# A fused cross-attention and mixture-of-experts layer: four engine programs written as one list each, in a new order

## What is computed

```python
x = x + xattn(layernorm(x), ctx, ctx, W_Q, W_K, W_V, W_O)   # 8 heads of 16
#   scores = q k^T / 4;  attn = softmax(scores, axis=1)       # over the HEADS
x = x + ffn(layernorm(x), Wr, br, W1, b1, W2, b2)
#   logits = x Wr + br; top 2 of 8; gates = softmax of the two
#   h = relu(x W1[e] + b1[e]);  y = sum_e gates[e] * (h W2[e] + b2[e])
```

## Time and profile before

| | before |
|---|---|
| median of 3 runs | 207.93 us (207.81 to 209.05) |
| profiled execution | 208.05 us |
| its span in the trace | 206.2 us |
| PE busy | 193.4 us (94%) |
| DVE busy | 171.9 us (83%) |
| ACT busy | 133.8 us (65%) |
| POOL busy | 120.1 us (58%) |
| granted TensorE clock | 90% or more of full in each of 40 slices |

### The profile page before, as it was taken

How to read it: one execution, slowest core, us unless ns; L and a number is a source line. 1 busy time by engine, 2 the same in 40 slices (tenths; PEclk the granted TensorE clock), 3 DMA queues, 4 the chain that set the end, 5 groups by cost and what they waited for, 6 DMA issues and landing times.

```text
span 206.2 us, 4730 instructions
## 1 busy us (share of the span) xinstructions
PE 193.4 (94%) x1600; PEld 170.7 (83%) x1600; DVE 171.9 (83%) x460; ACT 133.8 (65%) x318; POOL 120.1 (58%) x154
## 2 busy tenths in 40 slices
PE   6999997989998999999999999998999899979995
PEld 6449965976987799978899789978997799779994
DVE  5799986999999989998898989897999979356543
ACT  6257768957776568766777776776667665444541
POOL 6123959998699729376944967196729773220010
PEclk9999999999999999999999999999999999999999
DMA  6968789345024505041242324140000000000000
GB/s 167 275 214 208 174 268 259 106 135 153 5 102 127 156 26 174 10 150 33 102 102 78 103 103 105 60 119 3 0 24 4 2 0 14 15 3 0 27 2 29
DMA packets 20360, 18.74 MB, mean 91 GB/s; under 512 B 1776, under 2 KB 18800, under 8 KB 20336
## 3 DMA queue, kind: packets, MB, share of 16 engines
q1 hardware_dynamic: 19904, 18.04, 30.6%
q10 hardware_dynamic: 432, 0.39, 0.6%
HBM read 11.88 MB, written 6.55 MB: 89 GB/s over the span
## 4 chain that ended last, share of the span: by engine, by line
PE 66%; DVE 19%; issue 7%; POOL 6%; ACT 1%; DVEq 0%; POOLq 0%; ACTq 0%
PE y_ps L449 20%; PE h_ps L434 12%; PE misc_ps L390 6%; PE score_ps L371 6%; DVE acc L1026 4%; PE h_ps L379 4%; DVE attn L943 4%; PE score_ps L359 3%; PE score_ps L348 2%; DVE shift_m L935 2%; PE score_ps L292 2%; PE score_ps L434 2%; DVE ln_stats L895 1%; POOL gatesD L1244 1%; PE misc_ps L399 1%
## 5 line engine op out<-in xcount | busy, mean ns | idle before, releaser
L703 ACT ACTIVATE hT<-h_ps,b_sb 128x256 f32<-128x256 f32 x118 | 49.4, 470 | 31.1 <-PE h_ps L434 31.1
L449 PE MATMUL y_ps<-w_sb,hT 128*128 128x128 f32 x508 | 67.7, 276 | 0.0
L449 PEld LDWEIGHTS y_ps<-w_sb,hT 128*128 128x128 f32 x508 | 62.8, 192 | 1.8 <-issue 0.7
L1212 POOL TENSOR_TENSOR half_sum<-e_sb 128x512 f32<-128x512 f32 x28 | 37.6, 1344 | 21.0 <-ACT e_sb L675 21.0
L943 DVE TENSOR_TENSOR attn<-e_sb,e_rcp 128x1024 f32<-128x1024 f32 x32 | 48.2, 1511 | 0.6 <-ACT e_rcp L686 0.6
L935 DVE TENSOR_REDUCE shift_m<-score_ps 128x128 fp32r<-128x1024 f32 x32 | 38.5, 1211 | 0.3 <-PE score_ps L348 0.3
L675 ACT ACTIVATE e_sb<-score_ps 128x1024 f32<-128x1024 f32 x32 | 32.6, 1022 | 7.9 <-PE score_ps L371 5.9
L434 PE MATMUL h_ps<-x1T_hi,w_lo 128*128 128x256 f32 x118 | 37.4, 320 | 0.2
L1026 DVE SCALAR_TENSOR_TENSOR acc<-y_ps,gates,acc 128x128 f32<-128x128 f32 x96 | 28.9, 342 | 7.7 <-PE y_ps L449 6.1
L434 PE MATMUL h_ps<-x1T_hi,w_hi 128*128 128x256 f32 x118 | 32.9, 281 | 0.0
L434 PE MATMUL h_ps<-x1T_lo,w_hi 128*128 128x256 f32 x118 | 31.9, 281 | 0.0
(11 more groups left out here) (122 smaller groups left out, 276.9 us busy)
## 6 DMA issues: line engine op xcount, KB each, us to landing
k_scratch<-k_parts SPq DMA_DIRECT2D x14, 256.0 KB, 2.6
k_stack<-k_scratch SPq DMA_DIRECT2D x14, 256.0 KB, 4.0
q_stack<-q_scratch SPq DMA_DIRECT2D x28, 128.0 KB, 2.7
q_scratch<-q_parts SPq DMA_DIRECT2D x7, 256.0 KB, 2.1
w_sb<-in_w SPq DMA_DIRECT2D x1, 1024.0 KB, 6.3
out_y<-y_out SPq DMA_DIRECT2D x7, 128.0 KB, 1.8
x_all<-in_x SPq DMA_DIRECT2D x1, 768.0 KB, 6.4
ctxT<-in_ctx_t SPq DMA_DIRECT2D x1, 640.0 KB, 7.2
```

The source lines that it names most:

```text
L449: mm = nc.tensor.matmul(product(j, t), hT[:, j % 2, c, t * P:(t + 1) * P], w2_sb[:, e * HC + c, :], start=(c == 0), stop=(c == HC - 1))
L703: op = nc.scalar.activation(hT[:, j % 2, c, :], hidden(j)[:, c * S:(c + 1) * S], ACT.Relu, bias=b1_sb[:, e * HC + c:e * HC + c + 1])
L1212: nc.gpsimd.tensor_tensor(half_sum[:], e[:, 0:HQ // 2], e[:, HQ // 2:HQ], ALU.add).then_inc(sum_step, 1)
```

## The change

Every engine's `beginning()` and `period()` are replaced by one list, `program()`, over all eight batches, and the places of steps within the lists differ. No step is added or taken away, and no step's own instructions change, apart from the places of the b2 addition:

```diff
-    PERIODS = B + 5
-    B2_AFTER = 2
+    B2_AFTER = (2, 4, 3, 3, 3, 2, 0, 5)
...
-                if e == B2_AFTER + 1:
+                if e == B2_AFTER[b] + 1:
                     dve.wait_ge(b2_added, b + 1)
...
-                dve.wait_ge(gated, E * b + B2_AFTER + 1)
+                dve.wait_ge(gated, E * b + B2_AFTER[b] + 1)
```

SP's list: the load of `w1` goes behind the stack loads of batch 1, that of the later contexts behind those of batch 2:

```diff
             sp.dma_start(wr_sb[:], wr).then_inc(small_in, 16)
-            sp.dma_start(w1_sb[:], w1.rearrange("e d h -> d e h")).then_inc(w1_in, 16)
             spill_k(1)
             spill_q(1)
             load_k_stack(1)
             load_q_stack(1)
-            sp.dma_start(ctxT[:, 3:B, :], ctx_t[3:B].rearrange("b d s -> d b s")).then_inc(ctx_rest_in, 16)
+            sp.dma_start(w1_sb[:], w1.rearrange("e d h -> d e h")).then_inc(w1_in, 16)
```

On PE, the calls around the last `attend_values`. Before, the last two periods put it between `expert_up(6, 3)` and `expert_down(6, 2)`; now it stands between `expert_up(6, 1)` and `expert_up(6, 2)`:

```diff
+                expert_down(6, 0)
+                expert_up(6, 1)
+                attend_values(7, logits_made, 7)
+                expert_up(6, 2)
+                project_out(7, heads_taken, 8)
+                expert_down(6, 1)
```

More of the change, by code:

```diff
@@ L615, in _ @@
+                expert_up(7, 7)
+                gated_b2(7, logits_made, 8)
+                expert_down(7, 6)
+                expert_down(7, 7)
             pe.wait_ge(ident_made, 1)
@@ new lines, in program @@
+                add_residual(3)
+                ln2(3)
+                transpose_gates(2)
+                add_expert(2, 1)
+                k_lo(6)
+                add_expert(2, 2)
+                normalize(4, 0)
+                head_max(5, 0)
+                head_max(5, 1)
+                add_expert(2, 3)
+                add_b2(2)
+                add_expert(2, 4)
+                normalize(4, 1)
+                normalize(4, 2)
+                x1T_low(3)
+                add_expert(2, 5)
@@ new lines, in program @@
+                add_expert(2, 6)
+                take_logits(3)
+                normalize(4, 3)
+                q_lo(6)
+                head_max(5, 2)
+                choose_experts(3)
+                head_max(5, 3)
+                add_expert(2, 7)
+                normalize(5, 0)
+                make_gates(3)
+                add_expert(3, 0)
+                add_expert(3, 1)
+                transpose_gates(3)
+                add_residual(4)
+                ln2(4)
+                normalize(5, 1)
@@ new lines, in program @@
+                k_lo(7)
+                add_expert(3, 2)
+                add_expert(3, 3)
+                normalize(5, 2)
+                add_b2(3)
+                add_expert(3, 4)
+                x1T_low(4)
+                head_max(6, 0)
+                head_max(6, 1)
+                take_logits(4)
+                add_expert(3, 5)
+                add_expert(3, 6)
+                q_lo(7)
+                choose_experts(4)
+                normalize(5, 3)
+                normalize(6, 0)
@@ new lines, in program @@
+                add_expert(3, 7)
+                make_gates(4)
+                head_max(6, 2)
+                transpose_gates(4)
+                add_expert(4, 0)
+                head_max(6, 3)
+                add_expert(4, 1)
+                add_residual(5)
+                ln2(5)
+                add_expert(4, 2)
+                add_expert(4, 3)
+                add_b2(4)
+                normalize(6, 1)
+                head_max(7, 0)
+                head_max(7, 1)
+                x1T_low(5)
@@ new lines, in program @@
+                transpose_gates(6)
+                add_residual(7)
+                ln2(7)
+                add_b2(6)
+                add_expert(6, 1)
+                add_expert(6, 2)
+                x1T_low(7)
+                add_expert(6, 3)
+                add_expert(6, 4)
+                add_expert(6, 5)
+                add_expert(6, 6)
+                take_logits(7)
+                choose_experts(7)
+                add_expert(6, 7)
+                make_gates(7)
+                add_expert(7, 0)
@@ L1186, in _ @@
             ln1_end(0, 0)
[L1187 to L1189 removed]
+            program()
         @block.gpsimd
```

878 lines of the change are left out of this document (539 added, 339 removed).

## The result

The change made no gain. Over 20 executions each, the changed kernel takes 209.44 us (median; 208.36 to 211.29) and the kernel before 208.51: ratio 1.0053, 95% interval 1.0032 to 1.0074, so half a per cent slower. The profiled execution took 208.75 us, its span is 206.9 us, and 1.85 us lie outside the span as before. The forecast was 200.0 us.

The account below looks back on a forecast made before the run. VectorE and TensorE, both nearly full, bound the kernel until batch 7's last `normalize`, then TensorE alone. 43.7 + 120 + 3.9 = 167.6 us; the tail gives span 198.2, plus 1.85 outside: 200.0 us, range 195.0 to 206.0.

Parts of the forecast that it names:

- Step 1: VectorE from batch 0's last `normalize` to batch 1's: stretch falls from 22.8 to 15.1 us, starting at about 28.6 us.
- M1: End of batch 1's last `normalize`: 49.0 us before, forecast 43.7 us.
- Step 2: From batch 1's last `normalize` to batch 7's: 120 us of VectorE work plus 3.9 us of waits, ending at 167.6 us.
- M7: End of batch 7's last `normalize`: 176.1 us before, forecast 167.6 us.
- So the work stays at about 120 us: VectorE's work between the last `normalize` of batches 1 and 7: work put off returns, about 3.0 us goes out.
- the other 3.9 us of waits: VectorE's waits for expert products, `project_out` and `q` between batch 1's and 7's last `normalize`: all kept.
- The bias: `add_b2` waiting for the gated bias: 3.2 us of VectorE waits go, and 1.0 us of TensorE idle in the tail.
- the waits only move: Rival: two nearly full engines hand each other every delay, so removed waits return elsewhere; 205.6 us, chance 0.22.
- TensorE's count: TensorE's list from `attend_values(1)` to `attend_values(7)`: 119 us against 123.9 us available, so 5 us to spare.
- Step 3: Tail from the last `attend_values` to TensorE's end: 27.4 us where 26.1 passed before; TensorE ends at 195.2 us.
- Step 4: `w1` load lands after 6.3 us; ACT waits up to 0.8 us, costed at nothing because VectorE's other work covers it.
- The collisions: Rival: `normalize` meets GpSimd head sums more often, slower above mean 1.93 us, worst case 213.2 us; chance 0.08.

Follow-up runs that it names:

- a_bias_late: Changed kernel with the bias chain's place undone (transposes of batches 3 to 6 close ahead of `add_b2`, `ln2_end` ahead of `block_gates`): 215.87 us, ratio 1.0388.
- a_pe_cut: Changed kernel with 4.8 us less TensorE work: experts 1, 2, 4, 5 of batches 3 to 7 skip the low-half x1T pass: 207.59 us, ratio 0.9971.
- a_nr_both2: Changed kernel, GpSimd head sums replaced by non-reading memsets of 3.26 us, plus a 0.4 us VectorE memset ahead of each of 28 `normalize`: 204.84 us, ratio 0.9847.
- a_max4: Changed kernel with `head_max` reading four of the eight heads, 16.9 us less of it on VectorE: 207.30 us, ratio 0.9948.

## Why the prediction was wrong

**Step 1 (M1 at 43.7 us) was near.** The start of the stretch was right: the two `head_max` begin at 28.56 us, 28.6 was said. The stretch took 44.95 - 28.64 = 16.3 us in place of 15.1. Waits were not the cause: the two listed there are 0.75 and 0.15 us, near the 0.7 us said. `onehot` took 0.94 us where it takes 0.19 undisturbed, and two cheap instructions that split the router's weights, some 0.4 us, had not been counted.

**Step 2 (M7 at 167.6 us) failed,** by 8.9 us: 1.3 from M1, 3.85 in the sentence "So the work stays at about 120 us", and 3.8 in the sentence on the other 3.9 us of waits, "I keep them all".

- *The bias.* "The wait goes on VectorE, and on TensorE" is right. No row of `add_b2` is left above, and TensorE's waits for `gatesD` fell from 3.6 us (five times, whole run) to 0.3 us (once). Set at 3.2 + 1.0 us in the sum, it is worth 6.4 us in the new order by `a_bias_late`.
- *The work.* VectorE's work from M1 to M7 is 123.85 us, from 118.93 counted in the same way. Of these 4.9 us more, 3.4 are `make_gates`: its first and third instruction took 3.63 + 2.26 us over six batches, before 1.28 + 1.17. The step took off 0.9 us "if `make_gates` runs without POOL beside it", and it runs beside GpSimd's sums in four of these six batches. Another 2.6 us are `add_expert`, of which 14 calls are followed straight by the next one in place of 5, and neighbouring calls cost more (below). Some smaller steps took less.
- *The waits.* They sum to 7.7 us in place of 3.9. That is what the rival "the waits only move" said; its price of 205.6 us was too low, since it put back at most the waits that had been removed. Of its mechanism, two full engines that hand each other every delay, `a_pe_cut` shows one direction: TensorE's waits for VectorE grow as its own work shrinks.
- *TensorE's count.* "That is 119 us, against 123.9 us" was off. Without reads, and with 0.2 us of its waits listed, TensorE takes 168.22 - 43.97 = 124.25 us from `attend_values(1)` to `attend_values(7)`. Its expert steps take 76.8 us there from start to start, where 74.5 were counted, and `scores` and `subtract_max` 23.2 in place of 20.2; the other terms held. The 5 us to spare were not there, and the span of 198 us that the forecast asked for is the one that this list reached with no late result from batch 1 on. So the forecast asked that nothing be late on a list without slack.

**Step 3 (the tail) was near.** From the start of `attend_values(7)` to the end of the span it is 206.9 - 177.07 = 29.8 us in place of 27.4 + 3.0 = 30.4, and TensorE has no wait in it. The 27.4 us were added to 26.1 us that the chain gave, and in TensorE's timeline the same stretch of before is 26.6 us long. In the changed kernel the timeline gives 203.76 + 0.61 - 177.07 = 27.3 us, so the tail grew by 0.7 us and not by 1.3.

**Step 4 (`w1`) was right.** ACT waits 0.6 us for it, at most 0.8 was said, although landing took 7.8 us in place of 6.3. The cover held: between 20.1 and 28.6 us VectorE has no wait in its timeline, with `head_max` and `normalize` back to back.

**The collisions** were set at 0.08, with a worst case counted from a mean `normalize` of over 1.9 us. The mean rose only from 1511 to 1549 ns, so by that test the rival was refuted, and the test was too narrow. It looked at one instruction's mean, while the small ones of `make_gates` and GpSimd's own sums were hit too, and it asked only for the growth, while the collisions already in the kernel before cost 4.6 us there. What the new order changed is what the collisions cost: 9.0 us in it, 4.2 us in the old order with the bias early, although the reads lengthen VectorE's instructions alike. Without them the excess falls by 10.9 us in the new order (23.1 to 12.2) and by 11.3 us in the old one (19.3 to 8.0). In the old order TensorE waits for nothing from 92 to 177 us; in the new one delays of VectorE still reach it there.

Without the reads, the new order meets the forecast's marks: M1 lies at 43.58 us and M7 at 167.70. That is luck as far as the parts go. VectorE has 114.5 us of work and 9.6 us of waits between them, where 120 and 3.9 were said, and the length of the stretch is that of TensorE's list.

The Trainium skill, page "SBUF — State Buffer", section "SBUF: two separate sides", says that an instruction that loses the port pair blocks until the other's end. The rows at 45.20 and 46.34 agree within 0.02 us. The same section of the Trainium skill says that a VectorE instruction with two SBUF inputs is affected only by a GpSimd instruction that reads SBUF. The mean `normalize` of 1256 ns without reads of the head sums agrees, and so do the two of these 32 that still took 1.71 and 1.76 us: GpSimd's split of `w1`, which reads, was under way as they began.

What stays open: which delays, besides that of `make_gates`, make up the half of the 9.0 us that `a_nr_both2` does not give back, and which places of the new order, one by one, make it wait where the old one does not. Ahead of the tail, neither VectorE's nor TensorE's amount of work alone sets its pace, as `a_max4` and `a_pe_cut` show.

## What to carry to other kernels

Before a reordering is costed by waits removed, count the busiest engine's own list to the end: if its sum is the forecast, the forecast holds only if nothing is ever late. Try a single edit that takes an engine's wait off the path (here the bias's transposes some steps earlier) alone first: it gained 4.5 us in the old order, and inside a new order of everything its gain was lost again. And test which engine sets the pace by taking a few microseconds off each: the share that comes back (0.88 of TensorE's in one order, 0.39 in the other, 0.06 to 0.14 of VectorE's) says more than busy shares, which are nearly the same in the two orders (94 and 95%, 85 and 85%).

## What the runs showed of the hardware

- A short VectorE instruction can pay as much for a GpSimd instruction that reads as a long one: 0.90 us in place of 0.16 for 128x2 numbers. With GpSimd's memsets in place of the head sums' reads, 28 of the 32 `normalize` took 1.21 to 1.23 us, but that short one (a tensor with a constant) still took 0.67 and 0.94 us in two batches where a memset was under way, until the end of the memset within 0.03 us.
- Two `add_expert` in a row start 0.71 us apart, and one followed by another kind leaves after 0.53 us. Both are in these VectorE rows of the changed kernel, with the second call adding to what the first wrote:

```profile
72.13 0.61 DVE L1216 SCALAR_TENSOR_TENSOR acc<-y_ps,gates,x 128x128 f32<-128x128 f32 x2
72.84 0.61 DVE L1216 SCALAR_TENSOR_TENSOR acc<-y_ps,gates,acc 128x128 f32<-128x128 f32 x2
73.37 1.21 DVE L1125 TENSOR_REDUCE shift_m<-score_ps 128x128 fp32r<-128x1024 f32 x1
```

- TensorE's clock is not always full. Four of the 20 executions of the changed kernel show a mean granted clock of 0.992 and took 210.4 to 211.3 us. In the profiled execution of `a_max4` the mean was 1.00 from 31 to 36 us, where TensorE was busy for 3.44 of 5.00 us, then 0.60 and 0.72 in the next two stretches of 5 us, where it was busy for 4.76 and 5.00. The levels are 2.4 and 1.2 GHz, so by these means it ran at the lower one for four fifths of the first and over half of the second:

```profile
31.00:36.00 5.00, 3.44 (x22) 2.56 (x20) 3.29 (x10) 3.70 (x8) 4.40 (x7) 1.00 1.03 304
36.00:41.00 5.00, 4.76 (x23) 4.49 (x23) 2.35 (x12) 3.25 (x9) 4.69 (x7) 0.60 0.06 16
41.00:46.00 5.00, 5.00 (x29) 4.55 (x29) 4.15 (x5) 3.14 (x10) 4.84 (x6) 0.72 0.30 105
```
